# Wide attention with probabilities transposed on VectorE and four row tiles, and a re-ordered product-key stage, in a twelve-block kernel

## What is computed

```python
q = split_heads(x @ Wq) * 64 ** -0.5            # 16 heads of 64
k, v = split(context @ Wkv)                     # 257 rows, plus one learned null row
attn = softmax(q @ concat(null_k, k).T)
out = (attn @ concat(null_v, v)) @ Wout         # (128, 32, 128)
out = layernorm(out) * ln_scale + ln_bias       # added to the stream
```

## Time and profile before

| | before |
|---|---|
| median of 3 runs | 4069.61 us (4067.66 to 4072.36) |
| the profiled execution | 4067.78 us, its span 4066.0 us |
| PE busy | 3440.8 us (85%), 26,798 matmul records |
| DVE busy | 2662.2 us (65%) |
| ACT busy | 1706.5 us (42%) |
| POOL busy | 1223.8 us (30%) |
| product-key loop | about 400 to 1180 us of the span |
| wide attention | about 2077 to 3566 us of the span |

### The profile page before, as it was taken

One profiled execution on the slowest core, in us unless ns is written; L12 is line 12 of the kernel. 1 busy time (PEld: TensorE's weight loads), 2 busy tenths in 40 slices (PEclk: granted clock), 3 DMA queues, 4 the chain that ended last, 5 costly groups with the idle time before them and its releaser, 6 DMA issues. The chain is left out here.

```text
span 4066.0 us, 81543 instructions
## 1 busy us (share of the span) xinstructions
PE 3440.8 (85%) x26798; PEld 2918.8 (72%) x26800; DVE 2662.2 (65%) x7388; ACT 1706.5 (42%) x4422; POOL 1223.8 (30%) x1672
## 2 busy tenths in 40 slices
PE   3886888888877888887889999999999999975666
PEld 2775777777765666645779999999999999834244
DVE  7674888888866888856435555555555455559776
ACT  1231666666645777755313333323333233313342
POOL 3553776666642333312200000000000000036042
PEclk8896999999988999988789999999999999968677
DMA  3000000000002222200121111111111111146000
GB/s 89 4 0 34 1 0 0 0 0 0 0 14 68 75 76 77 68 11 6 33 57 47 44 47 48 48 42 47 47 48 45 45 43 47 38 87 89 0 3 24
DMA packets 263508, 147.67 MB, mean 36 GB/s; under 512 B 111476, under 2 KB 259912, under 8 KB 262760
## 3 DMA queue, kind: packets, MB, share of 16 engines
q1 hardware_dynamic: 259048, 142.13, 13.2%
q10 hardware_dynamic: 4352, 4.20, 0.5%
HBM read 131.82 MB, written 13.65 MB: 36 GB/s over the span
## 5 line engine op out<-in xcount | busy, mean ns | idle before, releaser
L920 PE MATMUL psum<-L_ffn_share,L_ffn_prob 128*128 128x128 f32 x4096 | 508.4, 283 | 141.9 <-DVE L_ffn_prob L849 141.9
L920 PEld LDWEIGHTS psum<-L_ffn_share,L_ffn_prob 128*128 128x128 f32 x4096 | 488.2, 197 | 174.3 <-DVE L_ffn_prob L849 142.2
L2134 ACT ACTIVATE L_xattn_prob<-psum,L_xattn_nmax 128x258 f32<-128x258 f32 x512 | 239.3, 473 | 674.3 <-DVE L_xattn_nmax L2169 674.3
L744 POOL TENSOR_TENSOR L_ffn_sums<-L_ffn_sims 128x1024 f32<-128x1024 f32 x256 | 485.7, 1912 | 106.0 <-DVE L_ffn_prob L849 105.7
L2246 PE MATMUL psum<-L_xattn_ctxT,L_xattn_q_ctx 128*128 128x257 f32 x2048 | 487.7, 380 | 0.0
L2284 PE MATMUL psum<-L_xattn_probT,L_xattn_ctx 128*128 128x256 f32 x2048 | 484.6, 379 | 1.7 <-DVE L_xattn_probT L2187 1.7
L2187 DVE COPY L_xattn_probT<-psum 128x512 f32<-128x512 f32 x256 | 177.1, 692 | 391.4 <-PE psum L2270 391.4
L849 DVE SCALAR_TENSOR_TENSOR L_ffn_prob<-L_ffn_sums,L_ffn_best,psum 128x512 f32<-128x512 f32 x512 | 358.8, 742 | 104.8 <-ACT psum L777 99.3
L2109 POOL TENSOR_TENSOR L_xattn_z_var<-L_xattn_z_mv,L_xattn_z_eps 128x1 f32<-128x1 f32 x32 | 6.1, 192 | 1397.3 <-DVE L_xattn_z_mv L2201 1364.5
L2246 PEld LDWEIGHTS psum<-L_xattn_ctxT,L_xattn_q_ctx 128*128 128x128 f32 x2048 | 370.1, 191 | 48.1
L2284 PEld LDWEIGHTS psum<-L_xattn_probT,L_xattn_ctx 128*128 128x128 f32 x2048 | 370.1, 190 | 42.2 <-ACT L_xattn_lastT L2145 2.2
(11 more groups left out here) (440 smaller groups left out, 6545.4 us busy)
## 6 DMA issues: line engine op xcount, KB each, us to landing
L_xattn_ctxT<-ctx_T_dram SPq DMA_DIRECT2D x128, 257.0 KB, 2.8
L_xattn_ctx<-ctx_dram SPq DMA_DIRECT2D x128, 256.0 KB, 3.0
L_xattn_k_all<-ctx_T_dram SPq DMA_DIRECT2D x128, 128.5 KB, 2.1
L_xattn_v_all<-ctx_dram SPq DMA_DIRECT2D x128, 128.0 KB, 2.2
L_attn_qkv_scratch<-L_attn_qkv SPq DMA_DIRECT2D x24, 256.0 KB, 2.8
L_attn_rows<-L_attn_qkv_scratch SPq DMA_DIRECT2D x24, 256.0 KB, 5.2
start_raw<-ctx_dram ACTq DMA_DIRECT2D x16, 256.0 KB, 12.1
start_plug_all<-plug_scratch SPq DMA_DIRECT2D x1, 2048.0 KB, 7.2
```

The lines of the kernel that those rows point to most:

```text
L744: nc.gpsimd.tensor_tensor(sums[:, h % RING, :, :], sx, sy, ALU.add).then_inc(summed, 1)
L920: last = nc.tensor.matmul(pair(2 * s)[:, c * P:(c + 1) * P], prob[:, h % RING, c * P:(c + 1) * P], share[:, h % RING, :], start=(h == 0 an ...
L2134: ins = nc.scalar.activation(prob[:, s, g, :], scores(s)[:, g, :], ACT.Exp, bias=nmax[:, s, g:g + 1], accum_out=total[:, s, g:g + 1])
```

## The change

In the product-key stage the normalised rows are made by ACT, from a shifted mean that POOL prepares behind head 6; the moments are taken behind head 2; `values` is issued before head 2, with a wait for `mixed`, and `output` behind head 3; the copy of the turned rows moves to head 2 on ACT.

In the wide stage the work goes by sequence, not by unit. DVE transposes the scaled probabilities in 32x32 blocks in SBUF. So 32 keys, not 128, lie on a quarter of the partitions for four heads each, and the context is mixed with 32-row matmuls in four row tiles, whose four groups of heads go to four PSUM banks. `ctx` therefore holds the context in eight blocks of 32 keys, once in each quarter of the partitions, loaded by four DMAs. The probabilities of the last keys are transposed by DVE too and pass through DRAM. Queries come in pieces of two heads in the upper halves of three banks. The 32 tiles are written out on PE, ACT, DVE and SP.

The diff, cut to its core:

```diff
--- product_key_experts, POOL
+            def normal_factors(t, s):
+                front.pool_rstd(pool, t - s, only=s)
+                pool.drain()
+                nc.gpsimd.tensor_scalar(shifted_mean[:, s:s + 1], front.mv[:, s, 0:1], front.rstd[:, s, :], -1.0, ALU.mult,
+                                        ALU.mult).then_inc(centred, 1)
...
-                    if after and h == 1:
-                        front.pool_rstd(pool, t + s, only=1 - s)
+                    if after == 2 and h == 6:
+                        normal_factors(t + 2, s)
--- ACT
+            def normalise(t, s):
+                act.wait_ge(centred, t + 1)
+                nc.scalar.activation(front.xn[:, s, :], core.x[:, ds(t, 1), :].rearrange("p a d -> p (a d)"), ACT.Identity,
+                                     bias=shifted_mean[:, s:s + 1], scale=front.rstd[:, s, :]).then_inc(front.normed, 1)
...
-                    if after and h == 1:
+                    if after and h == 2:
                         front.act_copy(act, t + s, only=1 - s)
...
+                    if after == 2 and h == 7:
+                        normalise(t + 2, s)
--- DVE
+                    if after == 2 and h == 2:
+                        front.dve_moments(dve, t + 2 - s, only=s)
...
-                    if after == 2 and h == 6:
-                        front.dve_moments(dve, t + 2 - s, only=s)
...
-                if after == 2:
-                    front.dve_normalise(dve, t + 2 - s, only=s)
--- PE
-                    if before and h == 2:
+                    if after and h == 1:
+                        pe.wait_ge(mixed, t)
+                        values(t + 1, o)
+                    if before and h == 3:
                         output(t - 1)
-                    if after and h == 2:
-                        values(t + 1, o)
--- wide_attention
+    mix_bank = lambda r: core.psum[:, 4 + r, 0:2 * P]
+    q_bank = lambda k: core.psum[:, 5 + k % 4 % 3, 2 * P:4 * P]
+    OUT = core.psum[:, 4, 2 * P:3 * P]
...
     def over_tiles(eng, tile):
-        tile(0, 0, False, 2)
-        with eng.Fori(0, TILES // 2 - 2) as it:
...
+        for t in range(TILES):
+            tile(t, t % 2, t > 0, min(TILES - 1 - t, 2))
--- SP
+            for r in range(G):
+                sp.dma_start(ctx[32 * r:32 * r + 32, b, :, :],
+                             row[0:2 * P, :].rearrange("(k m) c -> m k c", m=32)).then_inc(ctx_in[b], 16)
...
-            sp.wait_ge(lastT_done, (t + 1) * UNITS)
+            sp.wait_ge(lastT_done, (t + 1) * BT)
+            sp.dma_start(last_dram, lastT[:, p, :, :].rearrange("p b n -> p (b n)")).then_inc(last_out, 16)
+            sp.wait_ge(last_out, (t + 1) * 16)
...
--- ACT
+            for b in range(BT):
+                following = next_seq(t, b, p, after)
+                if following:
+                    for s in range(2):
+                        exps(following[0] * BT + following[1], s)
+                act.wait_ge(mixed, t * BT + b + 1 + BT)
+                nc.scalar.copy(mixed_ctx[:, :, :, b * SEQ:(b + 1) * SEQ],
+                               core.psum[:, 4:8, 0:2 * P].rearrange("p r (x n) -> p r x n", n=SEQ)).then_inc(mix_out, 1)
--- DVE
+        def turn(t, b, p, s):
+            n = t * BT + b
+            dve.wait_ge(exped, 2 * n + s + 1)
             nc.vector.reciprocal(total[:, s, :], total[:, s, :])
             dve.drain()
             for g in range(2):
                 nc.vector.tensor_scalar(prob[:, s, g, 0:2 * P], prob[:, s, g, 0:2 * P], total[:, s, g:g + 1], None, ALU.mult)
...
+            dve.drain()
+            if s == 0:
+                dve.wait_ge(mixed, n - 1 + BT)
+            nc.vector.transpose(probT[:, b % 2, :, 2 * s:2 * s + 2, :].rearrange("p k g n -> p g k n"),
+                                prob[:, s, :, 0:2 * P].rearrange("p g (k m) -> p g k m", m=32)).then_inc(turned, 1)
+            if s == 1:
+                nc.vector.transpose(lastT[:, p, b, :], tail[:, :]).then_inc(lastT_done, 1)
...
         def tile(t, p, before, after):
+            for b in range(BT):
+                following = next_seq(t, b, p, after)
...
+                if following:
+                    maxes(*following[0:2], 0)
+                if before and b == 0:
+                    add_up(t)
+                for piece in q_pieces(t, b, p, after):
+                    q_copy(*piece)
+                if following:
...
+                    turn(*following, 0)
+                    maxes(*following[0:2], 1)
+                    turn(*following, 1)
--- PE
+        def mix(t, b):
+            pe.wait_ge(turned, 2 * (t * BT + b) + 2)
+            for c in range(2):
+                for k in range(KB):
+                    for r in range(G):
+                        rows = slice(32 * r, 32 * r + 32)
+                        last = nc.tensor.matmul(mix_bank(r)[:, c * P:(c + 1) * P], ctx[rows, b, k, c * P:(c + 1) * P],
+                                                probT[rows, b % 2, k, :, :].rearrange("p g n -> p (g n)"), start=(k == 0),
+                                                stop=(k == KB - 1))
+            last.then_inc(mixed, 1)
...
         def tile(t, p, before, after):
+            for b in range(BT):
+                following = next_seq(t, b, p, after)
+                if following:
+                    score(*following, 0, True)
+                if before and b == 0:
+                    output(t - 1)
+                if before or b:
+                    pe.wait_ge(mix_out, t * BT + b)
+                pieces = q_pieces(t, b, p, after)
+                for piece in pieces[0:3]:
+                    q_piece(*piece[0:2])
+                if following:
+                    score(*following, 1, True, range(0, 1))
+                for piece in pieces[3:4]:
+                    q_piece(*piece[0:2])
+                if following:
+                    score(*following, 1, True, range(1, 2))
+                if pieces:
+                    pe.wait_ge(q_out, t * PIECES + 4 * b + PIECES + 8)
+                if before and b == 0:
                     pe.wait_ge(z_copied, t)
...
+                mix(t, b)
```

270 lines of the change are left out of this document (108 added, 162 removed).

## The result

| | before | after |
|---|---|---|
| median | 4068.64 us (4066.11 to 4072.36, 4 runs) | 3899.82 us (3889.69 to 3910.36, 4 runs) |
| ratio | | 0.9586, 95% interval 0.9563 to 0.9609 |
| profiled execution, its span | 4067.78, 4066.0 us | 3910.36, 3908.2 us |
| product-key loop | 794.6 us | 699.5 us |
| wide attention | 1519.7 us | 1451.1 us |

The change made the kernel 169 us faster; the forecast was 3885, 15 us off. The stage lengths are taken between the ends of PE's blocks in the trace. Both touched stages became shorter, by 95 us and by 69; the mixing block behind the wide attention, whose code is the same, took 4.6 us more; the other stages moved by 1.5 us or less. The profiled execution is the slowest of the four after, 10 us above their median, so differences between traces and between medians need not be equal.

A forecast was written before the change was run, and what follows sets the result against it. The prediction took TensorE to bound the wide stage and a ring of waits the product-key stage. It summed 4067.8 - 102 - 83 = 3882.8, with the median 1.8 us above: 3885 us, range 3825 to 3990 for 8 in 10.

The forecast's parts named there:

- Product-key tile: Layer 0 product-key experts: a tile falls from 24.1 to 20.8 us, -102 us over 31 tiles (-56 to -136).
- three signs: Product-key stage: ACT's wait for `values` under 1 us, no 1.85 us DVE op, a new DVE wait before the add to x.
- The normalise leaves DVE (-1.85 us of its 20.52): Product-key tile: moving the normalisation to ACT cuts DVE's busy time from 20.52 to 18.7 us.
- Moments go to head 2, so POOL waits for nothing there: Product-key tile: with moments taken at head 2, POOL has no wait for them; no separate time was given.
- POOL is busy beside it here: Product-key tile end: remark that POOL works during DVE's 1.85 us normalisation, called long beside a similar op.
- Wide tile: Layer 2 wide attention: a tile falls from 46.5 to 43.9 us, -83 us over 32 tiles (-141 to nothing).
- changes of tiling: Wide attention: switching PE between full array and row tiles costs 0.2 us each, two per sequence, +0.4 us.
- Rival (b): Wide mix: four row tiles don't run fully at once, 3.07x instead of 4x, +135 us, 4020; chance 0.12.
- Rival (a): DVE or handshakes eat part: slow wide transpose (+40) or product-key tile at 22.3 us (+46), 3925 to 3970; chance 0.17.
- Rival (c): Wide mix: PE's instructions don't arrive fast enough, slower than before, 4315 us at the densest long stretch's pace; chance 0.08.
- (d): Wide mix: row tiles run one after another, 1,350 us more; chance 0.01.
- Writing it out removes nothing: Wide attention: PE has no idle time, so the loop around the tiles costs nothing and unrolling it gains nothing.

The follow-up runs named there:

- e1_pk_only: The kernel before with only the product-key part of the change: 3967.93 us, ratio 0.9758.
- e6_two_maxima: The changed kernel with DVE's maximum over half of the wide scores taken twice, 1.4 us more DVE work per sequence: 3912.41 us.
- e3_loop: The changed kernel with the wide tiles in a loop of two again, first and last three written out: 4014.95 us.
- e12_pool_shift: The changed kernel with DVE's add to x moved behind the seventh head's bests and the shift subtraction given to POOL: 3833.16 us.
- e5_four_changes: The changed kernel with each sequence's mix cut in two, so PE changes tiling four times instead of twice: 4091.9 us.

## Why the prediction was right, and where not

- **Product-key tile.** Forecast 20.8 us, measured 21.12 to 21.23, and -102 us against -95 (-101 by the medians of e1_pk_only). The size was right. Its three signs came: ACT has no wait left for `values`, the long DVE operation is gone, and the new wait before the add to x is 1.16 us (0.8 forecast). The reason given for the size was partly wrong. "The normalise leaves DVE (-1.85 us of its 20.52)" priced an operation that was waiting for POOL; taken alone it is worth 8 us (14 by the stage lengths), not 57. The order of `values` and `output` is worth 31. Per tile the normalisation gave 0.57 us, the order 1.1 and the early moments 1.4, where the prediction took 1.85 for the first and nothing for the last. That its sum came out near 3 us is in part luck. Half of the gain, 48 us, is in a step that got half a sentence and no price, "Moments go to head 2, so POOL waits for nothing there": POOL's 2.87 us, and the clock. The prediction noted that "POOL is busy beside it here" beside the 1.85 us and did not ask which other operations of DVE the new order would bring beside POOL. L833 went from 0.23 to 0.98 us for it.
- **Wide tile.** Forecast 43.9, measured 44.34, 2.28 us less than the 46.62 of before, where 2.6 was forecast. The changes of tiling were right, 0.20 us each. A round of four takes 0.112 us for 0.11 taken, so the mix without its changes 3.57 for 3.52, 0.2 us per tile, and the two tail matmuls, 0.22 us per tile, were in no term. In the stage that is -69 us for -83: 10 of the 14 us are the tile's, and PE's waits for its code, 6.7 us, were in no term either.
- **Rival (b)**, four row tiles that run at 3.07 of 4: no. A round of four in 0.112 us is the pace of one 128-column record over the whole array (the output projection, 64 in 7.14 us between starts), and within 4% of half the 256-column pace. The figure of the Trainium skill (TensorE: Matmul & The Clock Gate, Part 3), given there for 512 columns, isn't seen here with 128.
- **Rival (a)**: the transpose took 0.71 us for 0.69, the query copy 0.41 for 0.43, and e6_two_maxima shows nearly 1.4 us of room.
- **Rival (c)** was right as a mechanism and wrong in its place and price. In one long stretch of code PE runs dry eight times in 1,380 us, under 7 us in all. At a jump back it does so each time. It was given 0.08 and (d) 0.01; the last paragraph of the prediction puts 0.09 on slower and 0.03 on no change, though only these two were to end there, so its 0.88 should have been 0.91.
- **"Writing it out removes nothing"** is true of the kernel before, and of no use for the one after. The prediction weighed the loop in the old kernel alone. With the new mix in the old loop the whole change would be worth 54 us (e3_loop) and not 169.
- **Not forecast**: the unchanged block behind the wide stage took 173.7 us before and 178.3 after. That goes with its granted clock. The windows of this block in the kernel before, in the kernel after and in e12_pool_shift, whose code is the same as after's from the wide stage on:

```profile
3567.00:3739.00 172.00, 120.79 (x1504) 78.19 (x1504) 128.12 (x290) 52.49 (x128) 100.20 (x167) 0.78 0.57 96
3402.00:3578.00 176.00, 124.22 (x1484) 79.92 (x1488) 127.98 (x291) 52.15 (x127) 100.15 (x167) 0.75 0.56 94
3333.00:3503.00 170.00, 115.44 (x1504) 75.71 (x1504) 128.37 (x291) 52.05 (x127) 99.94 (x167) 0.84 0.58 97
```

  With the same code the block takes 172 us at 0.84 and 178.3 at 0.75, and the other variants lie between. So these 5 us are no cost of the new code. What sets the clock there isn't shown.

The two misses of the sum, 7 us and 14, and the 5 us of that block have the same sign, and make up 26 of the 28 us between the sum of 3882.8 and the profiled 3910.4; the median lies 10 us below that execution. That the last 5 us point the same way is chance.

## What to carry to other kernels

An operation of DVE that is far longer than its like may be waiting, not working: look whether an instruction of POOL ends just before it (here 0.08 us), and move or give away the operation rather than count its time as work. Price a loop by the code of the new body, not of the old one, and write out only the engine that runs dry. Where a small instruction stands in the order of a busy engine and waits for another, price the wait and not the instruction.

## What the runs showed of the hardware

- DVE's operations from SBUF to SBUF (a tensor_scalar of 128x128 and a tensor_tensor of 128x64) ended 0.08 us after POOL's running sum in each of the four places shown; eight maxima (L831) took 1.10 us and two masks with one operand in PSUM (L866) 1.40 beside the same sums, as long as without them.
- A change between whole array and four row tiles costs PE 0.20 us, by two more changes in e5_four_changes (0.41 us) and by the starts around a mix (about 0.4 us for two).
- Four row tiles of 32x128 in float32 ran 16 rounds of four in 1.79 us, 0.112 us per round and 28 ns per record, the pace of a single 128-column record over the whole array.
- PE waited 2.9 us at the jump back of a loop with 2,824 loads and matmuls, and 1.3 to 1.5 us twice more in each turn; with 1,192 it did not; in straight code of the same instructions it waited for them under 7 us in 1,380.
- PE's granted clock fell to its lower level of 1.2 GHz (0.53 in the mean of the window) behind 2.62 us of idle time that followed 1.52 us shortly before, and 16 records took 3.68 us instead of 2.05. In another tile 2.52 us of idle behind 1.63 left it at 1.00, so these rows give no condition.
